# A graph network layer in 52 units of 40 steps: three jobs of the unit boundary put into earlier steps

## The chip, the cores and the metric

The kernel runs on one core of one Trainium2 chip. The metric is the device time of one launch in microseconds (us). Five engines of the core take part, each with its own instruction stream: PE (the matrix engine), ACT (activations), DVE (elementwise work), POOL (it starts the gathers) and SP (it starts the other transfers). Streams meet only in semaphores: an instruction waits until a counter has reached a number, and everything behind it on its engine waits with it.

## What is computed

One gated graph layer over 12,500 nodes with 128 features and 400,000 edges sorted by their destination. Cut to what matters:

```
h = relu(layernorm(x))
att = sigmoid(h[src] @ W_att[:d] + h[dst] @ W_att[d:] + b_att)
messages = (h[src] @ W_msg + b_msg) * att
aggregated = segment_sum(messages, dst, num_segments=num_nodes)
gi = aggregated @ W_ih.T + b_ih;   gh = h @ W_hh.T + b_hh
r = sigmoid(i_r + h_r);  z = sigmoid(i_z + h_z);  n = tanh(i_n + r * h_n)
h_new = (1 - z) * n + z * h
out = x + gamma * (h_new - mean) * rsqrt(var + BN_EPS) + beta
```

## The kernel before

**Stages.** A first part normalizes x, makes a table of messages and scores per node (98 tiles of 128 nodes, kept in SBUF as `m_all`), and sorts out the edges. A long middle, in units, sums messages and makes the new states. A last part applies the batch norm and stores.

**Two ways of summing.** The edges of the first 5,972 destinations go a tile of 128 edges at a time (1,520 tiles): POOL gathers the rows of the sources, ACT makes their gates (`gate(t)`, L928), DVE masks them to a window of destinations (`mask(t)`, L1217), PE multiplies (`scatter(t)`, L1491). The other 51 blocks of 128 destinations go "dense": ACT makes a gate for every pair of a source tile h and the block's destinations (`dense_gate`, L932, 98 tiles per block, into one of two large buffers), PE builds counts of edges from one-hot rows (`build`, L1501, sixteen pair groups per block), DVE multiplies gates by counts (`keep_pairs`, L1243, sixteen per block), and PE sums 98 products over the whole table (`block_part`, L1506; each shows as two MATMUL rows). DVE then copies the block's sum out of PSUM (`keep_block`, L1249, into `agg_blk`).

**Jobs.** A cell job turns 128 summed nodes into new states: six products on PE (`gru`, L1512 to L1515, twelve rows), two sigmoids on ACT (`gru_rz`, L937, L938), two operations on DVE (`gru_u`, L1254, L1257), a tanh on ACT (`gru_n`, L942), four operations on DVE (`gru_new`, L1262 to L1268). There are 51 dense jobs and 47 of gathered nodes. All use one PSUM bank, so that PE's products of a job wait until `gru_u` of the job ahead has read its own.

**Units and steps.** The middle is 52 units of 40 steps. Every engine runs through the same units and steps by its own loop, and tables of steps say what it does where; no engine waits for another at a step's end, so they are at different steps at one time. In unit u, PE builds the counts of block u and sums block u - 1. The order within a step is that of the code. What stands at the end of a unit and at the start of the next, before the change:

- PE: parts of block u - 1 in the 36 steps from `PARTS_AT` = 3 on, to step 38. Builds in steps 0, 2, 5, 7, ... 35, 37. A tile's `scatter` in about three steps of four, none in step 0. Cell jobs start in the steps of `GRU_AT` = (2, 10, 18, 26, 33); the dense one is in the first of these five places, a gathered one mostly in the fifth. The first part waits for all sixteen `keep_pairs` of its block and for the copy of the sum before it.
- DVE: `keep_pairs` of group 14 in step 39 and of group 15 in step 1 of the next unit, right behind the copy `keep_block`. `gru_u` of the fifth place's job (`U_AT` = 40) in step 0 of the next unit, behind step 0's other work.
- ACT: gates of the next block in steps 7 to 39 and 0 to 2 (`DENSE_AT` = 7, 36 parts), so none in steps 3 to 6. Part i of the gates waits until PE has summed part i of the block that used the buffer before: at step 7 + i ACT waits for what PE does at step 3 + i.
- SP loads keys, scores and h rows behind what frees their buffers, and in the last two units parts of x as the parts of the sum free the large buffers.

The planner gives the fifth place a job in 40 of the 52 units; units 0, 1, 2, 6, 14, 18, 25, 29, 33, 41, 45 and 51 have none there. Below, a crossing is the stretch from the last product of a block to the first of the next; "with a job" means that the unit that ends there had one in the fifth place (39 crossings between sums), "jobless" that it had none (ten, into units 2, 3, 7, 15, 19, 26, 30, 34, 42 and 46).

Of the kernel before, what the change touches and what calls it, by code (L numbers as in the profile page):

```python
# [19 lines left out]
BLOCKS = 51  # L20
UNITS = BLOCKS + 1
STEPS_U = 40
# [11 lines left out]
BEATS = PAIRS_B // BATCH  # L34
PER_BEAT = STEPS_U // BEATS
PARTS = 36
PARTS_AT = 3
DENSE_AT = 7
SET_LAG = 2
ADDED_LAG = SET_LAG + GROUPS_S  # L40
GRU_AT = (2, 10, 18, 26, 33)
RZ_AT = (8, 16, 23, 32, 39)
U_AT = (10, 18, 25, 34, 40)
N_AT = (13, 21, 28, 37, 43)
# [21 lines left out]
def tile_at(u, s):  # L66

    t = tiles_before(u, s)
    return t if tiles_before(u, s + 1) > t else None
# [22 lines left out]
def gru_jobs(steps):  # L92

    jobs, at, gathered = [], {}, 0
    for u in range(UNITS):
        for slot, s in enumerate(GRU_AT):
            if slot in ((4,) if u == BLOCKS else (1, 3)):
# [41 lines left out]
def gnn_program(nc, x, src, dst, W_msg, b_msg, W_att, b_att, W_ih, b_ih, W_hh, b_hh, gamma, beta, out):  # L139
# [30 lines left out]
    assert TILES % 2 == 1 and SPARSE < TILES and FINE <= P and GROWS <= P and HI <= P and 5 * GROWS <= 512 and KEYS <= 256  # L170
    assert SPARSE % SET == 0 and GROUPS % 2 == 0 and DENSE_AT + PARTS < STEPS_U + 4 and NEW_BACK_AT > NEW_AT[0] and PARTS_AT + PARTS < STEPS_U and SETS > 2 and TILES % 16 == 5
    assert QCOLS == 2 * QHALF and (FINE + 1) * QHALF <= 512 and FINE * P <= QCOLS * P
# [18 lines left out]
    with ExitStack() as ctx:  # L191
# [288 lines left out]
        def group_bases(first, n, engine):  # L480
            _, values = nc.values_load_multi_w_load_instructions(
                group_at[0:1, bass.ds(first, n)], engines=[engine], min_val=0, max_val=D0,
                skip_runtime_bounds_check_because=BOUNDED)
            return list(values)

        def set_ready(engine, k):

            engine.wait_ge(set_loaded[k % 2], 16 * (2 + GROUPS_S) * (k // 2 + 1))

        def keys_ready(engine, b):  # L490

            engine.wait_ge(keys_loaded[b % 2], 32 * (b // 2 + 1))
# [17 lines left out]
        def job_at(u, s, steps):  # L510

            for slot, step in enumerate(steps):
                v = u - (step // STEPS_U)
                if s == step % STEPS_U and (v, slot) in JOB_AT:
                    return JOB_AT[v, slot]
            return None
# [13 lines left out]
        def _(sp):  # L530
# [115 lines left out]
            def load_x_again(c):  # L646
                if width_of(c) == CHUNK:
                    sp.dma_start(x_again[:, c * TPC:(c + 1) * TPC, :], x_rows(c)).then_inc(x_back, 16)
                else:
                    for j, n in tiles_of(LAST):  # L650
                        sp.dma_start(x_again[0:n, c * TPC + j, :], x[c * CHUNK + j * P:c * CHUNK + j * P + n, :]
                                     ).then_inc(x_back, 16)

            def free_part(b, end):

                h = -(-(end - (LN_AT, KEY_AT)[b % 2]) // P)
                return next(i for i in range(PARTS) if slices_of(i, HI).stop >= h)

            def x_parts(b, s):

                chunks = range(X_EARLY) if b == BLOCKS - 2 else range(X_EARLY, CHUNKS)
                return [c for c in chunks if free_part(b, X_AT + (c + 1) * CHUNK) + PARTS_AT == s]

            for u in range(UNITS):
# [6 lines left out]
                for s in range(STEPS_U):  # L671
# [10 lines left out]
                    for c in x_parts(u - 1, s) if u >= BLOCKS - 1 else ():  # L682
                        sp.wait_ge(block_parts, PARTS * (u - 1) + s - PARTS_AT + 1)
                        load_x_again(c)
# [339 lines left out]
        def _(dve):  # L1024
# [184 lines left out]
            def next_batch(u, beat):  # L1209

                b, batch = (u, beat + 1) if beat + 1 < BEATS else (u + 1, 0)
                return (b, batch) if b < BLOCKS else None
# [14 lines left out]
            def set_bases(k):  # L1227

                return group_bases(k * GROUPS_S, GROUPS_S, ENGINE.DVE)

            def keep_set(k):

                dve.wait_ge(tiles_summed, (k + 1) * SET)
                wait_reuse(dve, groups_added, k * GROUPS_S)
                nc.vector.tensor_copy(lanes[:, :], ps[:, SP_BANK, 0:GROUPS_S * WIN]).then_inc(sums_kept, 1)
# [9 lines left out]
            def keep_block(b):  # L1245
                dve.wait_ge(block_parts, b * PARTS + PARTS)
                if ("dense", b - 1) in JOBS:
                    dve.wait_ge(gru_summed, JOBS.index(("dense", b - 1)) + 1)
                nc.vector.tensor_copy(agg_blk[:, :], ps[:, AM_BANK, 0:P]).then_inc(block_kept, 1)  # L1249
# [27 lines left out]
            for u in range(UNITS):  # L1277
                builds = u < BLOCKS
                for s in range(STEPS_U):
                    beat, i = s // PER_BEAT, s % PER_BEAT  # L1280
                    t = tile_at(u, s)
                    if t is not None:
                        if t % SET == 0:
                            set_ready(dve, t // SET)
                        if t % SET == SET_LAG - 1 and t > SET:
                            keep_set(t // SET - 1)
                        mask(t)
                        if t > SET and SET_LAG <= t % SET < ADDED_LAG:
                            of = t % SET - SET_LAG
                            add_group((t // SET - 1) * GROUPS_S + of, bases[of])  # L1290
                    if u == BLOCKS and s == LAST_TILES + SET_LAG:
                        keep_set(SETS - 1)
                        for of, base in enumerate(bases):
                            add_group((SETS - 1) * GROUPS_S + of, base)
                    if s == 1 and u > 1:
                        keep_block(u - 2)
                    if i == 1 and beat and builds:
                        keep_pairs(u, 2 * beat - 1)
                    if s == 1 and u:
                        keep_pairs(u - 1, 2 * BEATS - 1)  # L1300
                    if builds and i in (2, 3) and next_batch(u, beat):
                        b, batch = next_batch(u, beat)
                        if i == 2:
                            if batch == 0:
                                keys_ready(dve, b)
                            wait_reuse(dve, pairs_built, u * (2 * BEATS) + 2 * beat)
                            lo_hots(b, batch)
                        else:
                            key_hots(b, batch)
                    if i == 4 and builds:  # L1310
                        keep_pairs(u, 2 * beat)
                    if t is not None and t % SET == SET - 1:
                        bases = set_bases(t // SET)
                    k = job_at(u, s, U_AT)
                    if k is not None:
                        gru_u(k, nodes_of(k)[1])
                    k = job_at(u, s, NEW_AT)
                    if k is not None:
                        gru_new(k, nodes_of(k)[1], new_at(k), entry_of(k))
                    if u == 0 and s == 20:  # L1320
                        dve.wait_ge(bad_summed, 1)
                        nc.vector.tensor_copy(bad_all[:, :], ps[0:1, 7, 0:1]).then_inc(bad_known, 1)
                    if u == 0 and STEPS_U - 8 <= s < STEPS_U:
                        if s == STEPS_U - 8:
                            dve.wait_ge(edges_kept, ALL_TURNED)
                            for half in range(2):
                                dve.wait_ge(dense_stored[half], 32)
                                dve.wait_ge(scores_stored[half], 16)
                        n = -(-(AGG_W - ZEROED) // 8)
                        first = ZEROED + (s - STEPS_U + 8) * n  # L1330
                        nc.vector.memset(agg[:, first:min(AGG_W, first + n)], 0.0).then_inc(agg_zeroed, 1)
                if u == 0:
                    dve.wait_ge(agg_zeroed, 8)
# [79 lines left out]
        def _(pe):  # L1413
# [116 lines left out]
            for u in range(UNITS):  # L1530
                for s in range(STEPS_U):
# [3 lines left out]
                    if u < BLOCKS and s % PER_BEAT in (0, 2):  # L1535
                        build(u, 2 * (s // PER_BEAT) + (s % PER_BEAT) // 2)
                    if u and s == PARTS_AT:
                        pe.wait_ge(pairs_kept, u * (2 * BEATS))
                        wait_reuse(pe, block_kept, u - 1)
                    if u and PARTS_AT <= s < PARTS_AT + PARTS:  # L1540
                        for h in slices_of(s - PARTS_AT, HI):
                            last = block_part(u - 1, h)
                        last.then_inc(block_parts, 1)
                    k = job_at(u, s, GRU_AT)
                    if k is not None:
# [68 lines left out]
```

## Time and profile before

| | |
|---|---|
| median of 3 runs | 2234.89 us (2234.73 to 2235.26) |
| the profiled execution | 2235.2 us, span of its instructions 2233.5 us |
| busy in the span | PE 2037.2 us (91%), DVE 2007.9 us (90%), ACT 1977.8 us (89%), POOL 1534.1 us (69%) |
| granted TensorE clock, mean | 0.967 |
| the units | from about 262 to 2202 us |

A share of the span is a mean over the three stages; in the middle all of PE, ACT and DVE are busier than that. A matmul's end in the trace is modelled, and matmuls are pipelined, so the starts of PE's rows tell more than their durations. Of ACT and DVE the rows of successive instructions overlap by some 0.1 us; the distance between starts is what one costs.

### The profile page before, as it was taken

How to read it: one execution, taken by the hardware profiler on the slowest of the kernel's cores; microseconds unless marked ns; L12 is line 12 of the kernel's file. 1: busy time of each engine (PE TensorE's matmuls, PEld its weight loads, DVE VectorE, ACT ScalarE, POOL GpSimd, SP SyncE). 2: the span in 40 equal slices, each digit the busy share in tenths (PEclk: the TensorE clock that was granted, in tenths of full speed). 3: DMA queues.
4: the chain of work that ended last, by engine and by line, in shares of the span. 5: the costliest groups of instructions: out<-in, count | busy, mean ns of one | idle time of the engine just before them, and what ended most of it. 6: DMA issues, size and time to landing. Idle time of an engine off the chain costs nothing.

```text
span 2233.5 us, 53581 instructions
## 1 busy us (share of the span) xinstructions
PE 2037.2 (91%) x18022; PEld 1975.7 (88%) x18022; DVE 2007.9 (90%) x4463; ACT 1977.8 (89%) x6922; POOL 1534.1 (69%) x1618
## 2 busy tenths in 40 slices
PE   4535999999999999999999999999999999999997
PEld 4524999999999999999999999999999999999997
DVE  4966989999999999999999999999999999999985
ACT  1369899999999999999999999999999999999944
POOL 4575776777777777777777777677777777777760
PEclk9765999999999999999999999999999999999999
DMA  6862222222222222223222232222222222222255
GB/s 159 231 186 65 59 59 63 64 62 64 64 65 62 62 63 63 63 60 65 62 63 62 63 65 61 64 63 64 64 64 62 63 63 61 67 60 63 61 163 182
DMA packets 169059, 174.20 MB, mean 78 GB/s; under 512 B 80657, under 2 KB 132675, under 8 KB 168531
## 3 DMA queue, kind: packets, MB, share of 16 engines
q0 software_dynamic: 51136, 105.61, 20.9%
q1 hardware_dynamic: 114852, 61.60, 10.9%
q10 hardware_dynamic: 2796, 3.56, 0.8%
q8 instruction: 145, 2.38, 0.5%
q14 instruction: 130, 1.06, 0.2%
HBM read 143.99 MB, written 26.62 MB: 76 GB/s over the span
## 4 chain that ended last, share of the span: by engine, by line
PE 35%; ACT 35%; DVE 23%; issue 6%; DMA 1%; ACTq 0%; DVEq 0%
ACT big L932 27%; PE ps L1506 20%; DVE big L1243 7%; ACT gate_ring L928 6%; PE ps L1491 6%; PE ps L1501 5%; DVE gate_ring L1217 3%; DVE key_hot L1202 3%; DVE lo_hot L1194 2%; PE ps L1512 1%; PE ps L1513 1%; DVE big L1160 1%; DVE big L1147 1%; DVE h_blk L1264 1%; DVE big L1405 1%
## 5 line engine op out<-in xcount | busy, mean ns | idle before, releaser
L804 POOL DMA_INDIRECT row_ring<-node_table,set_idx x1520 | 1446.5, 952 | 578.8 <-issue 322.8
L932 ACT ACTIVATE big<-set_score,big 128x128 f32<-128x128 f32 x4998 | 1607.2, 394 | 82.6 <-PE ps L1506 82.2
L1506 PE MATMUL ps<-big 128*128 128x128 f32 x9996 | 1422.8, 281 | 0.0
L1506 PEld LDWEIGHTS ps<-big 128*128 128x128 f32 x9996 | 1238.9, 192 | 0.0
L1243 DVE TENSOR_TENSOR big<-ps,big 128x784 f32<-128x784 f32 x816 | 787.1, 965 | 8.8 <-ACT big L932 5.2
L1491 PE MATMUL ps<-gate_ring,row_ring 128*128 128x64 f32 x3040 | 541.5, 263 | 74.3 <-DVE gate_ring L1217 64.6
L1491 PEld LDWEIGHTS ps<-gate_ring,row_ring 128*128 128x128 f32 x3040 | 464.0, 194 | 117.6 <-DVE gate_ring L1217 99.8
L1217 DVE SCALAR_TENSOR_TENSOR gate_ring<-lane,set_rel,gate_ring 128x64 f32<-128x64 f32 x1520 | 420.7, 278 | 123.7 <-ACT gate_ring L928 117.8
L928 ACT ACTIVATE gate_ring<-set_win,row_ring 128x64 f32<-128x64 f32 x1520 | 506.6, 341 | 21.6 <-DMA row_ring<-node_table,set_idx 17.7
L1501 PE MATMUL ps<-key_hot,lo_hot 128*128 128x196 bf16 x3264 | 418.0, 251 | 17.2 <-DVE key_hot L1202 9.7
L1202 DVE TENSOR_TENSOR key_hot<-ps,set_key 128x1568 bf16<-128x1568 bf16 x408 | 393.6, 965 | 0.0
L1501 PEld LDWEIGHTS ps<-key_hot,lo_hot 128*128 128x128 bf16 x3264 | 310.2, 110 | 23.6 <-issue 20.5
L1194 DVE TENSOR_TENSOR lo_hot<-ps,set_lo 128x1024 bf16<-128x1024 bf16 x408 | 278.0, 681 | 6.9 <-DMA set_key<-dense_key 6.9
L1512 PE MATMUL ps<-h_blk,gates 128*128 128x128 f32 (+1 forms) x392 | 79.5, 286 | 0.5 <-DVE agg_blk L1249 0.5
L1462 PE MATMUL ps<-ident,big 128*128 128x128 f32 x98 | 20.5, 344 | 52.4 <-DVE big L1160 52.4
L883 ACT ACTIVATE big<-ps 128x512 f32<-128x512 f32 (+1 forms) x25 | 14.7, 589 | 55.4 <-issue 26.3
L1462 PEld LDWEIGHTS ps<-ident,big 128*128 128x128 f32 x98 | 13.7, 174 | 56.1 <-DVE big L1160 38.6
L1512 PEld LDWEIGHTS ps<-h_blk,gates 128*128 128x128 f32 x392 | 61.8, 199 | 0.7 <-issue 0.6
L937 ACT ACTIVATE n_blk<-ps,small 128x128 f32<-128x128 f32 (+1 forms) x98 | 34.4, 351 | 25.7 <-PE ps L1515 22.3
L1471 PE MATMUL ps<-big 128*128 128x130 f32 x196 | 36.6, 346 | 10.5 <-ACT big L883 10.4
L789 POOL DMA_INDIRECT big<-in_dst_dram,big x26 | 26.0, 1001 | 29.3 <-DVE big L1072 21.7
L942 ACT ACTIVATE n_blk<-n_blk,b_gates 128x128 f32<-128x128 f32 (+1 forms) x98 | 38.9, 397 | 6.5 <-DVE n_blk L1257 6.5
(131 smaller groups left out, 940.9 us busy)
## 6 DMA issues: line engine op xcount, KB each, us to landing
row_ring<-node_table,set_idx POOLq DMA_INDIRECT x1520
big<-in_x_dram SPq DMA_DIRECT2D x48, 256.0 KB, 6.0
h_blk<-hT_spill SPq DMA_DIRECT2D x97, 64.0 KB
node_table<-big SPq DMA_DIRECT2D x24, 258.0 KB
hT_spill<-big SPq DMA_DIRECT2D x24, 256.0 KB
out_dram<-big SPq DMA_DIRECT2D x24, 256.0 KB
set_win<-dst_scores SPq DMA_DIRECT2D x152, 32.0 KB
set_score<-dst_scores SPq DMA_DIRECT2D x51, 64.0 KB
```

What stands on the lines that cost most here:

```text
L804: nc.gpsimd.indirect_dma_start(row_ring[:, t % ROWS_RING, :], None, table, bass.IndirectOffsetOnAxis(ap=set_idx[:, t // SET % 2, t % SET:t ...
L928: nc.scalar.activation(gate_ring[:, t % GATES_RING, :], set_win[:, t // SET % 2, t % SET // GROUP, :], ACT.Sigmoid, bias=row_ring[:, t % R ...
L932: return nc.scalar.activation(a_buf[b % 2][:, h, :], set_score[:, b % 2, :], ACT.Sigmoid, bias=m_all[:, h, D:ROW])
L942: nc.scalar.activation(n_blk[:, 0:w], n_blk[:, 0:w], ACT.Tanh, bias=b_gates[:, 2:3]).then_inc(n_done, 1)
L1194: nc.vector.tensor_tensor(lo_hot[:, batch % 2, :, :, :], ps_lane_lo.bitcast(BF16).rearrange("p (l w) -> p l w", w=2).unsqueeze(1).broadcas ...
L1202: nc.vector.tensor_tensor(key_hot[:, batch % 2, :, :, :], ps_lane_key.bitcast(BF16).rearrange("p (h w) -> p h w", w=2).unsqueeze(1).broadc ...
L1217: nc.vector.scalar_tensor_tensor(out=hot, in0=lane[:, :], scalar=set_rel[:, t // SET % 2, t % SET:t % SET + 1], in1=hot, op0=ALU.is_equal, ...
L1243: nc.vector.tensor_tensor(a, ps_quad(q), a, ALU.mult).then_inc(pairs_kept, 1)
L1491: nc.tensor.matmul(ps_window(g), row_ring[:, t % ROWS_RING, 0:D], gate_ring[:, t % GATES_RING, :], start=t % GROUP == 0, stop=t % GROUP == ...
L1501: last = nc.tensor.matmul(ps_pairs(q, j), lo_hot[:, batch % 2, t // 2, :, t % 2], key_hot[:, batch % 2, t, :, :], start=True, stop=True)
L1506: return nc.tensor.matmul(ps[:, AM_BANK, 0:P], m_all[:, h, 0:D], a_buf[b % 2][:, h, :], start=h == 0, stop=h == HI - 1)
L1512: nc.tensor.matmul(both, gates[:, 3 + g, :], h, start=True, stop=False)
```

## The change

Four edits. The 36 parts start in step 2 instead of 3 and end in step 37. The first place of the cell jobs is step 0 instead of 2. `keep_pairs` of group 15 is in step 0 instead of 1. `keep_block` is in step 39 of the unit that sums the block, at the end of the step, instead of step 1 of the next.

```diff
-PARTS_AT = 3
+PARTS_AT = 2
...
-GRU_AT = (2, 10, 18, 26, 33)
+GRU_AT = (0, 10, 18, 26, 33)
...
-                    if s == 1 and u > 1:
-                        keep_block(u - 2)
                     if i == 1 and beat and builds:
                         keep_pairs(u, 2 * beat - 1)
-                    if s == 1 and u:
+                    if s == 0 and u:
                         keep_pairs(u - 1, 2 * BEATS - 1)
...
                     if t is not None and t % SET == SET - 1:
                         bases = set_bases(t // SET)
+                    if s == STEPS_U - 1 and 0 < u < BLOCKS:
+                        keep_block(u - 1)
                     k = job_at(u, s, U_AT)
                     if k is not None:
                         gru_u(k, nodes_of(k)[1])
```

ACT's and POOL's streams stay as they are, and the list of cell jobs and of who does what in which place stays too. On SP one load of a part of x in the second last unit stands one place earlier.

DVE at the crossing into unit 21, from step 38 on. `lo_hot` and `key_hot` are the one-hot rows, `big<-ps,big` with 98x8 is `keep_pairs`, `gate_ring` the mask of a tile. Before:

```order
L1202 TENSOR_TENSOR key_hot<-ps,set_key 128x1568
L1217 SCALAR_TENSOR_TENSOR gate_ring<-lane,set_rel,gate_ring 128x64
L1243 TENSOR_TENSOR big<-ps,big 128x98x8
L1254 SCALAR_TENSOR_TENSOR n_blk<-ps,b_gates,n_blk 128x128
L1257 TENSOR_TENSOR n_blk<-ps,n_blk 128x128
L1217 SCALAR_TENSOR_TENSOR gate_ring<-lane,set_rel,gate_ring 128x64
L1249 COPY agg_blk<-ps 128x128
L1243 TENSOR_TENSOR big<-ps,big 128x98x8
L1217 SCALAR_TENSOR_TENSOR gate_ring<-lane,set_rel,gate_ring 128x64
L1194 TENSOR_TENSOR lo_hot<-ps,set_lo 128x1024
```

DVE at the same place after the change:

```order
L1202 TENSOR_TENSOR key_hot<-ps,set_key 128x1568
L1217 SCALAR_TENSOR_TENSOR gate_ring<-lane,set_rel,gate_ring 128x64
L1243 TENSOR_TENSOR big<-ps,big 128x98x8
L1249 COPY agg_blk<-ps 128x128
L1243 TENSOR_TENSOR big<-ps,big 128x98x8
L1254 SCALAR_TENSOR_TENSOR n_blk<-ps,b_gates,n_blk 128x128
L1257 TENSOR_TENSOR n_blk<-ps,n_blk 128x128
L1217 SCALAR_TENSOR_TENSOR gate_ring<-lane,set_rel,gate_ring 128x64 x2
L1194 TENSOR_TENSOR lo_hot<-ps,set_lo 128x1024
```

The copy and the last `keep_pairs` now stand ahead of `gru_u` and of the masks of steps 1 and 2.

PE at the same crossing, from step 37's tile on before the change (`ps<-big` are parts of the sum, `key_hot,lo_hot` a build, `h_blk` and `agg_blk` the dense cell job). Before:

```order
L1491 MATMUL ps<-gate_ring,row_ring 128x64
L1501 MATMUL ps<-key_hot,lo_hot 128x196 x4
L1506 MATMUL ps<-big 128x128 x3
L1491 MATMUL ps<-gate_ring,row_ring 128x64
L1506 MATMUL ps<-big 128x128 x3
L1491 MATMUL ps<-gate_ring,row_ring 128x64
L1501 MATMUL ps<-key_hot,lo_hot 128x196 x4
L1491 MATMUL ps<-gate_ring,row_ring 128x64 x2
L1501 MATMUL ps<-key_hot,lo_hot 128x196 x4
L1512 MATMUL ps<-h_blk,gates 128x128
```

and then the other products of the job, a tile and five parts. After, again from step 37's tile:

```order
L1491 MATMUL ps<-gate_ring,row_ring 128x64
L1501 MATMUL ps<-key_hot,lo_hot 128x196 x4
L1506 MATMUL ps<-big 128x128 x3
L1491 MATMUL ps<-gate_ring,row_ring 128x64 x2
L1501 MATMUL ps<-key_hot,lo_hot 128x196 x4
L1512 MATMUL ps<-h_blk,gates 128x128
L1513 MATMUL ps<-agg_blk,gates 128x128
L1512 MATMUL ps<-h_blk,gates 128x128
L1513 MATMUL ps<-agg_blk,gates 128x128
L1514 MATMUL ps<-h_blk,gates 128x128
L1515 MATMUL ps<-agg_blk,gates 128x128
L1491 MATMUL ps<-gate_ring,row_ring 128x64 x2
```

and then a build and two parts. Ahead of the job stand the tiles of steps 38 and 39 and one build, behind it the tiles of steps 1 and 2 and the other build; the same pieces as before lie between the last and the first part, in another order.

## Rows read from the trace of the kernel before

**Rows 1.** The source view of the copy, L1249: its engine's idle time.

```profile
L1249 DVE COPY agg_blk<-ps x51: 281/283/293, 261.6 to 2201.7; 128x128 f32<-128x128 f32 x51
...
  PE ps L1506: 6.0, 2
```

**Rows 2.** Five stretches, 300 to 2130 us: sum of busy time by engine.

```profile
sum 1830.00, PE 1768.62 PEld 1726.76 DVE 1712.72 ACT 1755.22 POOL 1316.52; mean PE 353.72 PEld 345.35 DVE 342.54 ACT 351.04 POOL 263.30
```

**Rows 3.** Waits from 300 to 2150 us: total us, times, longest.

```profile
ACT big L932 <- PE ps L1506: 74.1, 49, 3.3
...
PE ps L1491 <- DVE gate_ring L1217: 48.4, 85, 1.0
```

**Rows 4.** DVE's timeline at a typical crossing (start, us, what, count, [idle before]).

```profile
885.39 0.35 DVE L1254 SCALAR_TENSOR_TENSOR n_blk<-ps,b_gates,n_blk 128x128 f32<-128x128 f32 x1
885.77 0.29 DVE L1257 TENSOR_TENSOR n_blk<-ps,n_blk 128x128 f32<-128x128 f32 x1
886.51 0.28 DVE L1217 SCALAR_TENSOR_TENSOR gate_ring<-lane,set_rel,gate_ring 128x64 f32<-128x64 f32 x1 [0.44 <-ACT gate_ring L928]
886.71 0.28 DVE L1249 COPY agg_blk<-ps 128x128 f32<-128x128 f32 x1
886.91 0.96 DVE L1243 TENSOR_TENSOR big<-ps,big 128x784 f32<-128x784 f32 x1
887.79 0.28 DVE L1217 SCALAR_TENSOR_TENSOR gate_ring<-lane,set_rel,gate_ring 128x64 f32<-128x64 f32 x1
```

**Rows 5.** PE's timeline at the same crossing, last part to first part.

```profile
885.22 0.89 PE L1506 MATMUL ps<-big 128*128 128x128 f32 x6
885.95 0.33 PE L1491 MATMUL ps<-gate_ring,row_ring 128*128 128x64 f32 x2
886.12 0.51 PE L1501 MATMUL ps<-key_hot,lo_hot 128*128 128x196 bf16 x4
886.85 0.43 PE L1491 MATMUL ps<-gate_ring,row_ring 128*128 128x64 f32 x2 [0.23 <-DVE gate_ring L1217]
888.12 0.43 PE L1491 MATMUL ps<-gate_ring,row_ring 128*128 128x64 f32 x2 [0.84 <-DVE gate_ring L1217]
...
890.27 1.33 PE L1506 MATMUL ps<-big 128*128 128x128 f32 x10
```

**Rows 6.** The timeline at a tight crossing, into unit 21.

```profile
1003.45 0.89 PE L1506 MATMUL ps<-big 128*128 128x128 f32 x6
...
1004.37 0.29 DVE L1249 COPY agg_blk<-ps 128x128 f32<-128x128 f32 x1
...
1007.94 1.33 PE L1506 MATMUL ps<-big 128*128 128x128 f32 x10
```

**Rows 7.** The chain that ended last, behind that crossing: PE comes back into it.

```profile
1020.72 0.43 PE ps L1491 x2
```

**Rows 8.** The timeline at a jobless crossing, into unit 30.

```profile
1351.68 0.89 PE L1506 MATMUL ps<-big 128*128 128x128 f32 x6
...
1352.15 0.97 DVE L1243 TENSOR_TENSOR big<-ps,big 128x784 f32<-128x784 f32 x1
...
1353.85 0.28 DVE L1249 COPY agg_blk<-ps 128x128 f32<-128x128 f32 x1
...
1354.39 0.33 ACT L928 ACTIVATE gate_ring<-set_win,row_ring 128x64 f32<-128x64 f32 x1
...
1354.93 0.27 DVE L1217 SCALAR_TENSOR_TENSOR gate_ring<-lane,set_rel,gate_ring 128x64 f32<-128x64 f32 x1
...
1357.94 0.69 ACT L932 ACTIVATE big<-set_score,big 128x128 f32<-128x128 f32 x2 [1.62 <-PE ps L1506]
```

**Rows 9.** PE at that crossing: its first part.

```profile
1357.23 0.61 PE L1506 MATMUL ps<-big 128*128 128x128 f32 x4
```

**Rows 10.** Windows with the granted clock (the 0.50 or 1.00 ahead of the DMA share).

```profile
301.75:305.16 3.41, 3.41 (x19) 3.41 (x18) 3.41 (x8) 0.64 (x3) 1.15 (x3) 0.50 0.42 58
...
2134.70:2138.12 3.42, 3.42 (x19) 3.38 (x19) 3.35 (x10) 1.06 (x5) 2.00 (x2) 0.50 0.18 39
```

## The prediction

> **What bounds the kernel now.** I read the page first. Its shares of the span (PE 91%, DVE 90%, ACT 89%) name no single engine, so I cut out the units: between 300 and 2130 us PE is busy 1768.6 of 1830 us, ACT 1755.2, DVE 1712.7 [rows 2], which leaves them 61, 75 and 117 us of idle time. One copy of a block's sum follows the other by (2201.7 - 261.6) / 50 = 38.8 us [rows 1]; that is the time of a unit. The view of waits then says where the idle time lies. ACT waited 49 times, once per crossing, for a part of PE's sum, 74.1 us in all, 1.5 us each; PE waited 85 times for a mask of DVE, 48.4 us in all [rows 3]. At the typical crossing PE's two waits of this kind are 0.23 and 0.84 us [rows 5]: 49 times 0.84 is 41 us, so that nearly all of PE's visible waiting stands at the crossings too.
>
> The timeline of one crossing shows the loop. PE's last part ends at 885.22 + 0.89 = 886.11 [rows 5]. DVE could not copy the sum then: it stood before the mask of step 1, which waited 0.44 us for ACT's gate; the copy came at 886.71, `keep_pairs` of group 15 at 886.91, the mask of step 2 at 887.79 [rows 4]. PE, idle 0.84 us, took that mask at 888.12, built, did the cell job and began the new sum at 890.27 [rows 5]. Only a part of that sum lets ACT go on with the gates of its step 7. Through all 51 copies DVE waited for PE's last part only twice [rows 1]; at the tight crossing the copy follows the end of the last part (1004.34) by 0.03 us [rows 6], at the typical one by 0.60. Behind the tight crossing the chain of work that ended last runs over DVE, and PE comes back into it only at 1020.72 [rows 7]: DVE is the late one for the first third of a unit. So the bound is a loop through all three engines, closed at the crossing, and no engine's throughput.
>
> **The change, crossings with a job (39).** Nothing is added or removed; every instruction is there before and after, and DVE's, PE's and ACT's work per unit stay the same. What moves is who waits. Let E be the end of a block's last part.
>
> Before, the first new part starts at E + 4.16 in the typical crossing (890.27 - 886.11) and at E + 3.60 in the tight one (1007.94 - 1004.34) [rows 5, 6]. Going through the crossings I count some ten of 39 at the tight end, so the mean is about 0.75 x 4.16 + 0.25 x 3.60 = 4.02.
>
> After, DVE reaches the copy early (its `keep_pairs` of group 14 was over by 885.39, when `gru_u` began [rows 4]) and has to wait for E. Then: copy at E + 0.03 [rows 6], group 15 0.20 later (886.71 to 886.91), the next instruction 0.88 later (886.91 to 887.79), and `gru_u` 0.38 + 0.29 until its end [rows 4]. That is E + 1.78. PE follows DVE's end by 0.05 (888.07 to 888.12) [rows 4, 5] and starts the cell job at E + 1.83. Behind the wait it has the same four pieces as before: job, two tiles, build. They took 890.27 - 888.12 = 2.15 [rows 5], of which up to 0.1 is the slow start of a product behind a wait; I take 2.10. The first new part starts at E + 3.93. The crossing itself gains 4.02 - 3.93 = 0.09 us. This is where the change looks larger than it is: the wait for a mask goes, but the dense job now stands behind `gru_u` of the job before it, through the shared PSUM bank, and `gru_u` now stands behind `keep_pairs` and the copy. Behind it on DVE are the masks of steps 1 and 2; PE needs them only after its job of some 1.4 us, so they cost nothing.
>
> A second term: where DVE is behind in the first third of a unit, PE stalls on masks. After the change DVE reaches any step later behind its copy by `gru_u` and one mask, 0.67 + 0.20 = 0.87 (0.20 is 886.51 to 886.71). PE reaches it later behind the copy by 3.90 - 3.56 (890.27 - 886.71) = 0.34 and by one more step of parts with its tile, 0.73 (885.95 - 885.22) and, three times in four, 0.17 (886.12 - 885.95) [rows 5], 0.86 in all. That is 1.2 against 0.87, so PE's stalls can shrink by 0.3. How long they are is not in one row, as the modelled ends hide up to 0.2 us of each; bounds 0 and 0.3, I take 0.25 since the chain runs through DVE there. Sum 0.34 x 39 = 13 us.
>
> **Jobless crossings (10).** Here no `gru_u` is in the way. In the one shown E is 1351.68 + 0.89 = 1352.57; DVE is free of group 14 at 1352.15 + 0.88 = 1353.03, so the copy is at 1353.03 instead of 1353.85. Group 15 follows at 1353.23, mask 1 at 1354.11, and mask 2 once ACT's gate is ready, at 1354.39 + 0.33 = 1354.72; with 0.04 until DVE starts and 0.28 for the mask PE goes on at 1355.1. Its job has by then been done, in the time in which it now waits; tile 0.17 and build 0.35 give the first part at 1355.6, against 1357.23 [rows 8, 9]. ACT's 1.62 us of waiting [rows 8] would vanish. But DVE's mask of step 2 is only 0.17 earlier (1354.76 against 1354.93), and PE, one step of parts further on (about 0.86), meets DVE in the first third of the unit: that lets 0.17 + 0.86 = 1.03 through. Between 1.03 and 1.62 I take 1.1, 11 us for ten.
>
> **The clock.** In five stretches of 3.41 us each, the first and last of which are shown, the granted clock was 0.50 [rows 10], the lower level of 1.2 GHz. Four of the five follow jobless crossings, after PE had stood nearly idle for longer than elsewhere. ACT's longest wait, at such a crossing, was 3.3 us [rows 3] instead of 1.62, so that one fall costs 1.7 us. With the cell job pulled into PE's gap of the jobless crossings these four should go: 4 x 1.7 = 7 us.
>
> **Costed at nothing.** The first and last units and the one x load that moves are taken as zero, within 2 us. The earlier copy needs PSUM's sum only, and `agg_blk` is free: the job that reads it was done in step 0.
>
> **The sum.** 13 + 11 + 7 = 31 us. The profiled execution is 2235.2 us, its span 2233.5; it is 0.3 above the median of 2234.89. 2235.2 - 31 = 2204 us.
>
> **Rivals.**
> - *Forecast, chance 0.54.* The terms at their bounds: crossings with a job 0 to 0.45 us each (0 to 18), jobless 1.0 to 1.6 (10 to 16), clock 3 to 8 (the fifth fall too). 2235 - 13 to 2235 - 42: 2193 to 2222.
> - *No difference, 0.16.* If most crossings behave like the tight one, where DVE already had the sum at once, the crossing with a job is longer by 3.93 - 3.60 = 0.33 us, 39 times 13 us, and what the jobless ones and the clock give back (18) is eaten up: 2231 us. For it: a kernel in which DVE waits for E each time has no slack left there. Against it: 0.60 us lay between E and the copy at the typical crossing.
> - *Slower, 0.13: the clock falls at the crossings with a job.* PE's waits there were two, 0.23 and 0.84, with a tile between [rows 5]. Afterwards they are one: it has two tiles and a build (until about E + 0.6) and then nothing until E + 1.83, 1.2 to 1.3 us. If the clock fell at each, 39 x 1.7 = 66 us, and the time is 2204 + 66 = 2270. It decides from 31 / 1.7 = 18 falls on. Against it: the typical crossing with its 1.1 us of waiting, and most with somewhat more, held 1.00, and the job's twelve products now break up the thin stretch. The Trainium skill ("TensorE: Matmul & The Clock Gate", "A second HAM failure mode: psum-queue depth-cycling") says that a matrix engine which idles briefly between groups of products again and again can swing between the two clocks. By that rule a regular gap at each unit would be this rival; the trace agrees only so far that the falls follow the longest gaps.
> - *Larger gain, 0.12.* ACT's wait of 74.1 us in 49 crossings [rows 3] is the ceiling of what the loop can give. If the stalls in the units shrink as well, and the loop closes on ACT's own work, 50 to 60 of it come: 2180 us.
> - The remaining 0.05 is for what I don't see, above all work near the sets' ends on DVE.
>
> **How the numbers follow.** What a measurement of this kernel can tell from no change is 0.2%, 4.5 us. Faster: the forecast, the larger gain, and a third of the second rival, 0.72. Same: most of the rest of that rival, 0.13. Slower: the clock and what I don't see, 0.15. The range takes in the larger gain and the weaker terms but not the clock: 2182 to 2228. The likeliest case's own is 2193 to 2222.
>
> **What would show it.** Right: DVE's copy waits for L1506 at nearly every crossing, 0.4 to 0.8 us each; PE's wait for a mask at the crossing is gone and one of about 1.3 us before L1512, put down to `gru_u` (L1257), stands there 39 times; ACT's wait for L1506 falls from 74 to about 45 us and is near zero at jobless crossings; the distance of copies is near 38.2 us; fewer than three windows of clock 0.50 within the units. Wrong: copies that start without waiting mean that DVE and not PE is last; stretches of 0.50 at the crossings with a job mean the clock; a wait of PE for masks in steps 7 to 18 longer than now means that DVE, later by 0.87 us, became the bound.

## The result and the profile after

The changed kernel took 2207.35 us in the median of 4 runs (2205.89 to 2207.76), the kernel before 2234.81 (2233.95 to 2235.26). The ratio is 0.9878, 95% interval 0.9866 to 0.9890: 27.5 us less. The forecast was 2204 in 2182 to 2228. The profiled execution has a span of 2205.5 us, 28.0 less than before.

The view of waits of the changed kernel, 300 to 2150 us (total, times, longest), answers to [rows 3]:

```profile
PE ps L1512 <- issue: 46.0, 40, 1.2
ACT big L932 <- PE ps L1506: 38.0, 45, 1.8
...
DVE agg_blk L1249 <- PE ps L1506: 15.8, 23, 1.6
PE ps L1491 <- DVE gate_ring L1217: 9.1, 34, 0.5
ACT n_blk L937 <- DVE bn_all L1268: 7.7, 12, 2.8
```

ACT's wait for a part of the sum went from 74.1 to 38.0 us, PE's wait for masks from 48.4 to 9.1. In their place stands a new one, 40 times before the first product of the dense job (L1512), 46 us in all. The view puts it down to "issue", that is to nothing it can see; the timeline below shows that the job starts 0.10 us after `gru_u` ends, and in the trace of e11_parts3 the view names `gru_u` (L1257) for the same wait.

The windows view, sum of five stretches from 300 to 2130 us, answers to [rows 2]:

```profile
sum 1830.00, PE 1765.57 PEld 1735.49 DVE 1731.93 ACT 1767.89 POOL 1336.97; mean PE 353.11 PEld 347.10 DVE 346.39 ACT 353.58 POOL 267.39
```

In the same 1830 us ACT and DVE are busy for 13 and 19 us more, PE's idle time is 64 us against 61. The engines do the same work in less time.

A crossing with a job, into unit 13, answers to [rows 4, 5]. The rows are from three timelines, of DVE, then PE, then ACT:

```profile
680.22 0.97 DVE L1243 TENSOR_TENSOR big<-ps,big 128x784 f32<-128x784 f32 x1
682.08 0.29 DVE L1249 COPY agg_blk<-ps 128x128 f32<-128x128 f32 x1 [0.89 <-PE ps L1506]
682.29 0.96 DVE L1243 TENSOR_TENSOR big<-ps,big 128x784 f32<-128x784 f32 x1
683.17 0.34 DVE L1254 SCALAR_TENSOR_TENSOR n_blk<-ps,b_gates,n_blk 128x128 f32<-128x128 f32 x1
683.55 0.29 DVE L1257 TENSOR_TENSOR n_blk<-ps,n_blk 128x128 f32<-128x128 f32 x1
...
681.19 0.86 PE L1506 MATMUL ps<-big 128*128 128x128 f32 x6
...
683.94 0.46 PE L1512 MATMUL ps<-h_blk,gates 128*128 128x128 f32 x2 [1.16 <-issue]
...
685.75 0.50 PE L1501 MATMUL ps<-key_hot,lo_hot 128*128 128x196 bf16 x4
...
686.82 0.69 ACT L932 ACTIVATE big<-set_score,big 128x128 f32<-128x128 f32 x2 [1.40 <-PE ps L1506]
```

The chain is the forecast one: last part over at E = 681.19 + 0.86 = 682.05, copy at E + 0.03, group 15 at + 0.24, `gru_u` over at + 1.79, cell job at + 1.89. There are 40 crossings of this kind, not 39: one into each of the units 4 to 51 that follows a unit with a job in the fifth place. The time from E to the first part is 4.04 us in their median (3.82 to 4.15), against 4.02 (3.29 to 6.43) before. It got no shorter, only uniform.

A jobless crossing, into unit 30 (DVE, then PE, then ACT), answers to [rows 8, 9]:

```profile
1335.35 0.96 DVE L1243 TENSOR_TENSOR big<-ps,big 128x784 f32<-128x784 f32 x1
1336.23 0.28 DVE L1249 COPY agg_blk<-ps 128x128 f32<-128x128 f32 x1
...
1337.96 0.29 DVE L1217 SCALAR_TENSOR_TENSOR gate_ring<-lane,set_rel,gate_ring 128x64 f32<-128x64 f32 x1 [0.38 <-ACT gate_ring L928]
...
1334.30 0.85 PE L1506 MATMUL ps<-big 128*128 128x128 f32 x6
...
1336.46 0.50 PE L1501 MATMUL ps<-key_hot,lo_hot 128*128 128x196 bf16 x4 [0.54 <-DVE big L1243]
1336.80 0.41 PE L1512 MATMUL ps<-h_blk,gates 128*128 128x128 f32 x2
...
1338.92 1.30 PE L1506 MATMUL ps<-big 128*128 128x128 f32 x10
...
1339.65 0.69 ACT L932 ACTIVATE big<-set_score,big 128x128 f32<-128x128 f32 x2
```

ACT goes on at its step 7 without any wait; before it had stood 1.62 us. The copy follows group 14 at once, as forecast.

The granted clock, in the first and the last of the five windows that make up the sum above:

```profile
300.00:700.00 400.00, 386.14 (x3563) 379.39 (x3562) 378.46 (x812) 388.97 (x1387) 291.80 (x309) 1.00 0.29 64
...
1900.00:2130.00 230.00, 221.39 (x2047) 217.72 (x2046) 217.91 (x467) 210.34 (x749) 169.52 (x179) 1.00 0.30 68
```

The third figure from the end, 1.00, is the clock. It is 1.00 in all five: none of the five stretches at 0.50 of [rows 10] is left between the first and the last sum.

**Where the 28 us came from.** Measured from the last part of one block to the last part of the next, that is over a crossing and the stretch of parts behind it, a unit behind a crossing with a job took 38.51 us in the mean before and 38.27 after (40 of them: 9.7 us), behind a jobless one 40.12 and 38.32 (ten: 18.0 us). The first block's last part came 0.3 us earlier. Ten of the fifty crossings thus gave two thirds of the gain.

### The profile page after: what moved, and what is told of

Same layout as the page of the kernel before. It is cut to its first block, busy times and chain, and to the rows that moved or that the text cites. A ratio compares the mean times of both kernels' runs of the same rounds, so it can differ in the third digit from the quotient of the medians.

```text
span 2205.5 us, 53581 instructions
## 1 busy us (share of the span) xinstructions
PE 2008.8 (91%) x18022; PEld 1961.2 (89%) x18022; DVE 2002.0 (91%) x4463; ACT 1980.0 (90%) x6922; POOL 1535.1 (70%) x1618
## 4 chain that ended last, share of the span: by engine, by line
PE 35%; ACT 34%; DVE 23%; issue 7%; DMA 1%; ACTq 0%; DVEq 0%
ACT big L932 25%; PE ps L1506 20%; DVE big L1243 6%; ACT gate_ring L928 6%; PE ps L1491 5%; PE ps L1501 5%; DVE key_hot L1202 3%; DVE gate_ring L1217 3%; DVE lo_hot L1194 2%; PE ps L1512 1%; PE ps L1513 1%; DVE big L1160 1%; DVE h_blk L1264 1%; DVE big L1147 1%; DVE big L1405 1%
## 5 line engine op out<-in xcount | busy, mean ns | idle before, releaser
L1506 PE MATMUL ps<-big 128*128 128x128 f32 x9996 | 1417.5, 281 | 0.0
L1506 PEld LDWEIGHTS ps<-big 128*128 128x128 f32 x9996 | 1236.5, 192 | 0.0
L1243 DVE TENSOR_TENSOR big<-ps,big 128x784 f32<-128x784 f32 x816 | 787.4, 965 | 9.6 <-ACT big L932 5.2
L1491 PE MATMUL ps<-gate_ring,row_ring 128*128 128x64 f32 x3040 | 516.0, 259 | 29.2 <-DVE gate_ring L1217 24.1
L1491 PEld LDWEIGHTS ps<-gate_ring,row_ring 128*128 128x128 f32 x3040 | 456.6, 194 | 53.3 <-DVE gate_ring L1217 45.3
L1512 PE MATMUL ps<-h_blk,gates 128*128 128x128 f32 (+1 forms) x392 | 79.0, 283 | 46.5 <-issue 46.0
L1512 PEld LDWEIGHTS ps<-h_blk,gates 128*128 128x128 f32 x392 | 59.3, 191 | 54.6 <-issue 54.6
L937 ACT ACTIVATE n_blk<-ps,small 128x128 f32<-128x128 f32 (+1 forms) x98 | 34.7, 354 | 31.1 <-PE ps L1515 23.3
```

What stands on the lines that cost most here:

```text
L1243: nc.vector.tensor_tensor(a, ps_quad(q), a, ALU.mult).then_inc(pairs_kept, 1)
L1491: nc.tensor.matmul(ps_window(g), row_ring[:, t % ROWS_RING, 0:D], gate_ring[:, t % GATES_RING, :], start=t % GROUP == 0, stop=t % GROUP == ...
L1506: return nc.tensor.matmul(ps[:, AM_BANK, 0:P], m_all[:, h, 0:D], a_buf[b % 2][:, h, :], start=h == 0, stop=h == HI - 1)
L1512: nc.tensor.matmul(both, gates[:, 3 + g, :], h, start=True, stop=False)
```

## The experiments

Two theories were put on record once the result was known, each time before the run that tests them. **T**: the chain over the crossing (last part, copy, group 15, `gru_u`, job, first part) sets the unit. **M**: the loop is longer; DVE's work *behind* the copy, up to where PE or ACT needs DVE in the new unit, then PE's parts up to the last one, sets it, and a shorter crossing alone gives nothing. The changed kernel agrees with both.

This table is worked out from the starts and ends of the parts (L1506) in the traces of the kernels below. A crossing runs from a block's last part to the next block's first, the stretch from there to that block's last part; means in us.

| | before | changed | e9_u39 | e10_u39first | e11_parts3 |
|---|---|---|---|---|---|
| with a job (40): crossing | 4.01 | 4.04 | 3.18 | 2.86 | 4.17 |
| the stretch behind it | 34.50 | 34.22 | 34.99 | 35.11 | 34.65 |
| both | 38.51 | 38.27 | 38.16 | 37.98 | 38.82 |
| jobless (ten): crossing | 5.43 | 3.87 | 3.90 | 3.89 | 3.67 |
| the stretch behind it | 34.68 | 34.45 | 34.45 | 34.46 | 35.10 |
| both | 40.12 | 38.32 | 38.35 | 38.35 | 38.77 |

The trace of e8_after, the changed kernel once more, has the means of "changed" within 0.03 us.

Of the twelve runs four fell on a chip on which the kernel before takes 2237 us, as in the comparison; eight fell on others, where it took 2618 to 2658 us, and where PE has many more waits that the trace puts down to nothing (last section). The four on the first chip decide; the others are told behind them.

### The four that decide: the changed kernel and three variants on one chip

**e8_after**, the changed kernel itself.

> The changed kernel itself, beside the kernel before on a chip of today, where the kernel before takes 2618 to 2658 us instead of 2235: PE's rows there show waits of 0.3 to 1.9 us put down to nothing, and the clock at 0.50 some 30 to 40 times within the units. If the crossing's chain is what the change works on, the crossings with a job stay near 4.0 us at the least and the jobless ones fall to about 3.5, and the ratio to before stays below 1, but by less than 1.2%, since PE's own waits now set most of the unit: 0.985 to 1.00.

Measured: 2206.77 us, ratio to before 0.9866 (0.9849 to 0.9882). The chip was not one of the slow ones, so that the condition in the text did not hold; the run repeats the result of the comparison.

**e9_u39**: `gru_u` of the fifth place in step 39, behind the copy.

```diff
-U_AT = (10, 18, 25, 34, 40)
+U_AT = (10, 18, 25, 34, 39)
```

> gru_u in step 39 behind the copy, on the same chip as e8_after. Theory T (the crossing's chain sets the unit): faster than e8_after by up to 0.9 us a crossing, 1.6% of the unit where no other wait covers it. Rival M (DVE's work behind the copy sets it): the least crossing falls to about 3.1 us, the time is that of e8_after within 0.3%.

Measured: 2202.65 us, ratio to before 0.9851 (0.9834 to 0.9867), 4 us below e8_after and within its interval. The least crossing is 2.94 us and the median 3.16, as expected, 0.88 below 4.04; had T held, 35 us would have gone. By the table the crossing is 0.86 us shorter in the mean and the stretch behind it 0.76 longer. Part of the reason is in the waits, 300 to 2150 us:

```profile
ACT n_blk L937 <- DVE bn_all L1268: 31.3, 39, 2.8
...
ACT big L932 <- PE ps L1506: 11.2, 23, 1.0
```

ACT's wait for the first part fell from 38.0 to 11.2 us, and its wait for DVE rose from 7.7 to 31.3: 45.7 together in the changed kernel, 42.5 here. L937 is the first sigmoid of the dense job, in step 8; it may not overwrite `n_blk` before `gru_new` of the job before (L1268, DVE's step 5) is through. PE meets DVE too: of its waits for masks, those between 10.5 and 16 us behind the first part are 2.6 us in all before the change, 6.8 in the changed kernel and 8.2 here. T falls. M stands, with the addition that DVE is met twice: by ACT at step 8, and by PE at its masks.

**e10_u39first**: the same, but `gru_u` ahead of the copy.

```diff
-U_AT = (10, 18, 25, 34, 40)
+U_AT = (10, 18, 25, 34, 39)
...
-                    if s == STEPS_U - 1 and 0 < u < BLOCKS:
-                        keep_block(u - 1)
                     k = job_at(u, s, U_AT)
                     if k is not None:
                         gru_u(k, nodes_of(k)[1])
+                    if s == STEPS_U - 1 and 0 < u < BLOCKS:
+                        keep_block(u - 1)
```

> gru_u in step 39 ahead of the copy, on the same chip. Theory T: faster than e9_u39 by 0.2 to 0.4 us a crossing. Rival M: faster than e8_after by up to 0.4 us a crossing, 0.7%, though e9_u39 is not.

Measured: 2196.4 us, ratio to before 0.9820 (0.9803 to 0.9836), 10.4 us below e8_after, 0.26 a job crossing. This is what M asks for: 0.67 us of DVE's work is put where DVE waited. Its waits:

```profile
ACT n_blk L937 <- DVE bn_all L1268: 34.2, 39, 2.8
...
DVE agg_blk L1249 <- PE ps L1506: 5.0, 11, 1.0
```

DVE's wait before the copy fell from 15.6 us (in e8_after) to 5.0, and that is the 10 us. M's own number, 0.4 us a crossing, took the mean wait of 40 crossings, but half of them have next to none to give. This kernel is faster than the changed one and than e9_u39.

**e11_parts3**: the changed kernel with the parts in steps 3 to 38.

```diff
-PARTS_AT = 2
+PARTS_AT = 3
```

> The parts in steps 3 to 38 again, the rest as changed, on the same chip. Theory T: 5 us slower than e8_after, 0.2%. Rival M: 0.8 us a unit slower, up to 40 us, 1.5%.

Measured: 2235.19 us, ratio to before 0.9991 (0.9981 to 1.0000): 28.4 us above e8_after. The crossing with a job grew by 0.20 us only in the median (to 4.24), which is T's share; crossing and stretch together grew by 0.55 in the mean. Its waits:

```profile
ACT big L932 <- PE ps L1506: 68.9, 55, 2.0
...
PE ps L1512 <- DVE n_blk L1257: 54.0, 39, 1.4
DVE agg_blk L1249 <- PE ps L1506: 32.6, 38, 1.3
```

The copy now waits for the last part 32.6 us instead of 15.6, since PE has one more step of parts behind the masks on which it met DVE. So the three other edits together give nothing measurable in the sum, and the gain appears with the first one.

In the sum only, for the table shows two parts that cancel. Against the kernel before, the three edits make a unit behind a jobless crossing 1.35 us shorter (40.12 to 38.77, ten: 13.5 us) and one behind a crossing with a job 0.31 us longer (38.51 to 38.82, forty: 12.3 us). The first edit then takes 0.55 us from each of the forty and 0.45 from each of the ten. The clock is 1.00 through the units of this kernel too, without any stretch at 0.50, so that what the four falls behind jobless units had cost is among the 13.5 us.

What the first edit gives alone is not known from this chip, and the move of the dense job to step 0 (`GRU_AT`) was run nowhere by itself. With the first edit each part also comes one step earlier against the gates with which ACT refills the buffer. That this is not the gain is argued only: e9_u39 takes most of ACT's wait for parts away and gets 4 us.

### On the slower chips

Their times are told as ratios to the kernel before on the same chip. In the order e4, e6, e1, e2, then e5, e7, then e12, e13, the kernel before itself took 2617.86 us there for the first four, 2658.32 and 2652.46 for the next two, 2657.56 for the last two.

**e4_u39**, the same kernel as e9_u39.

> The changed kernel, with gru_u of the fifth place's job in step 39, right behind the copy, instead of step 0 behind keep_pairs of group 15. Theory T (the chain over the crossing sets the unit: end of the last part, copy, group 15, gru_u, cell job, first part, 4.04 us): group 15 leaves the chain, the crossing falls by 0.9 to about 3.1 us, and 39 crossings give up to 35 us: 2172 to 2180. Rival M (the loop is set by DVE's work between the copy and the masks of about step 15, where PE stalls 13 us behind the first part, and by PE from there to the last part): DVE's work behind the copy is the same, so the crossing gets shorter and the stall longer by as much; 2200 to 2207.

Measured: 2619.62 us, ratio 1.0010 (0.9997 to 1.0024). **e7_u39again**, once more:

> The same kernel as e4_u39 (gru_u of the fifth place's job in step 39, behind the copy), once more, since PE's rows of the first runs show waits of 0.3 to 1.2 us for nothing that the profile names, which neither kernel had in the traces of the comparison. Theory T (the chain over the crossing sets the unit): the crossing falls from 4.04 to about 3.1 us and the time to 2172 to 2180. Rival M (DVE's work behind the copy sets it): the crossing falls as well, but PE's stall 13 us behind the first part grows by as much; 2200 to 2207.

Measured: a single execution of each, 2657.12 against 2652.46 us, too little for a verdict. **e5_u39first**, the same kernel as e10_u39first:

> The changed kernel, with gru_u of the fifth place's job in step 39 ahead of the copy, so that DVE does it in the time in which it waits for the last part. Behind the end of the last part stand only the copy and group 15, and the cell job's products need no waiting: theory T, the crossing falls from 4.04 to about 2.9 us, 39 x 1.1 = up to 40 us: 2167 to 2180. Rival M (the loop runs over DVE's work behind the copy to the masks of about step 15, and PE from there): DVE's work behind the copy is shorter by gru_u's 0.67 us, of which the time in which it now waits for the last part (0.4 us in the mean) is free: 39 x 0.4 = 16 us, 2188 to 2195, with a longer stall of PE 13 us behind the first part.

Measured: 2647.39 us, ratio 0.9964 (0.9949 to 0.9978). **e6_parts3**, the same as e11_parts3:

> The changed kernel, but the parts of the sum are in steps 3 to 38 again; the other three edits stay. Theory T: only the tile of step 3 is added to the crossing, 0.13 us x 40 = 5 us: 2212. Rival M: behind the mask at which PE stalls it has one more step of parts until the last part, about 0.8 us per unit, so up to 31 us: 2225 to 2238.

Measured: 2652.12 us, ratio 1.0140 (1.0122 to 1.0159). The order of the variants is the one found above (`gru_u` first, `gru_u` behind the copy, parts in step 3), the distances to the kernel before are not: all are some 1.5% worse against it than on the other chip. The changed kernel was not run there; whether its gain holds on such a chip is open. If it stood to these variants as on the other chip, its ratio would be about 1.00, an estimate from these three distances, and nothing of the gain would be left.

**e1_copy39**: the kernel before with only the copy moved.

```diff
-                    if s == 1 and u > 1:
-                        keep_block(u - 2)
...
+                    if s == STEPS_U - 1 and 0 < u < BLOCKS:
+                        keep_block(u - 1)
```

> The kernel before, with nothing but the copy moved to the end of step 39. DVE then waits for the last part ahead of gru_u, the mask of step 1 and group 15. The mask of step 2 comes about 0.3 us later at a typical crossing and 0.9 later at a tight one: about +0.45 x 39 = 18 us, 2245 to 2260, by both theories. If DVE's order at the crossing did not matter: 2235.

Measured: 2636.06 us, ratio 1.0074 (1.0057 to 1.0090), 18 us slower.

**e2_pairs0**: the kernel before with only group 15 in step 0.

```diff
-                    if s == 1 and u:
+                    if s == 0 and u:
```

> The kernel before, with nothing but keep_pairs of group 15 moved to step 0. DVE does it in the time in which it waited 0.44 us for the gate of step 1, so all that follows comes about 0.45 us earlier: -0.45 x 39 and 0.17 x 10, about -19 us, 2216, by both theories. If only the whole set of edits helps: 2235.

Measured: 2614.7 us, ratio 0.9986 (0.9974 to 0.9999): 3 us less, at most 7 by the interval, where 19 were expected. The signs of both are the expected ones, and the loss of e1_copy39 has its size; but with PE's own waits in every unit neither number can be carried to the other chip.

**e12_parts2**: the kernel before with only `PARTS_AT = 2`.

```diff
-PARTS_AT = 3
+PARTS_AT = 2
```

> The kernel before with nothing but the parts in steps 2 to 37; copy and group 15 stay in step 1, the dense job in step 2, now behind that step's parts. Theory M (the loop of DVE's work behind the copy, PE from the mask of about step 15 to the last part): PE has one step of parts less behind that mask, -0.8 us a unit, DVE has 0.87 us less behind the copy than in the changed kernel, and the job's 1.36 us leave the crossing, which falls from 4.0 to about 2.7: the loop loses more than in the changed kernel, until ACT's own work (1.4 us a unit below the time before) stops it: 2175 to 2205. Rival S (the four edits need each other, since the part in step 2 waits for the copy and group 15 of step 1 on DVE): no better than the kernel before, 2225 to 2240.

Measured: 2666.37 us, ratio 1.0037 (1.0022 to 1.0052). **e13_parts2_pairs0**, with group 15 in step 0 as well:

> As e12_parts2, with group 15 in step 0 as well, so that DVE does it while it would wait for the gate of step 1. Theory M: up to 0.4 us a unit below e12_parts2, less where ACT's work already sets the unit: 2170 to 2200 and not slower than e12_parts2. Rival S: this one gives what e12_parts2 does not, 2205 to 2215.

Measured: 2652.16 us, ratio 0.9979 (0.9964 to 0.9993). Both numbers look like rival S, which says that the first edit needs the others. It is not shown: between the first and the last copy of a sum the granted clock was at 0.50 in 51 and 43 stretches, against 28 to 42 in the others of these chips and none in the four that decide, and the kernel before has no trace there. Nor is the 0.50 a full answer, since e1_copy39 has 42 such stretches, nearly as many as e13_parts2_pairs0. Whether the earlier parts alone would do on an undisturbed chip stays open.

## Why the prediction was right, and where it was not

**The bound.** "A loop through all three engines, closed at the crossing, and no engine's throughput" held, but not as "closed at the crossing": e9_u39 and e10_u39first show that the loop runs on behind it.

**Crossings with a job.** The chain was right instruction by instruction: 1.83 us to the cell job forecast, 1.89 measured; 2.10 for the rest, 2.15. The sum was 3.93 against a measured 4.04, so that the term of -0.09 us a crossing came out as +0.02. The prediction counts the same four pieces of PE in every crossing; that holds for the typical one, but in 16 of the 40 a tile less stood there before, and in one after, so that 0.38 tiles of 0.17 us moved into the crossing in the mean. The warning of that step, that the wait for a mask goes and one for `gru_u` comes, is the 46.0 us at L1512. The prediction's 39 should be 40, which changes its sum by 0.3 us.

**The second term, -0.25 us** (PE's stalls on masks behind the crossing). The stretch behind these crossings got 0.27 us shorter in the mean (34.50 to 34.22), of which 0.06 is the tile that left it. So the size is right, and part of the reason: one step of parts less behind DVE's masks. But the prediction made it a side term and gave the crossing the space, and e11_parts3 shows that without this edit a unit is 0.55 us longer. Nor did all stalls shrink: PE's waits for masks outside the crossings rose from 3.6 to 7.9 us, most of them 11 to 15 us behind the first part. That is the last of the signs named as "wrong", DVE late in steps 7 to 18. It came, at a size that cost nothing in the sum.

**Jobless crossings.** Forecast 11 us and 7 for the clock, 1.8 us each; measured 18.0 in ten, 1.80 each. ACT's wait is gone as said: 1.60 to 1.74 us at the six without a fall of the clock, 0 to 0.23 after. These six gained 1.24 us each (0.6 to 2.0), near the forecast 1.1, but not by the way described: the first part was to start at E + 3.03 (1355.6 - 1352.57) in the one shown and started at E + 3.77, because the build ahead of the job waited 0.54 us for a `keep_pairs` (L1243) and the job was not done when mask 2 was. The crossings of the six gave 0.94 us in the mean instead of some 1.6, the stretches behind them 0.30. That the two errors meet near 1.1 is in part luck.

**The clock.** All five falls went. The price of 1.7 us can be read from the trace of before. Into unit 19, with the clock at 0.50, and into unit 30, at 1.00, PE goes from the same tile through build and job to its first part:

```profile
926.60 0.69 PE L1491 MATMUL ps<-gate_ring,row_ring 128*128 128x64 f32 x2 [0.97 <-DVE gate_ring L1217]
...
930.26 1.33 PE L1506 MATMUL ps<-big 128*128 128x128 f32 x10
...
931.02 1.30 ACT L932 ACTIVATE big<-set_score,big 128x128 f32<-128x128 f32 x4 [3.25 <-PE ps L1506]
...
1355.26 0.43 PE L1491 MATMUL ps<-gate_ring,row_ring 128*128 128x64 f32 x2 [0.84 <-DVE gate_ring L1217]
```

That is 3.66 us against 1.97 (first part at 1357.23, [rows 9]), 0.17 of it for one tile more: 1.5 us for the clock. ACT's waits at the four such crossings are 3.23 to 3.27 us against 1.60 to 1.74. Of this about 1.4 us reached the unit: the four gained 2.63 us each, the six others 1.24, and 4 x 1.4 is 5.6 us where 7 was forecast. In e11_parts3 the difference is the same, 2.27 against 0.73. The fifth fall was at a crossing with a job, into unit 50, whose unit gained 1.1 us where the other 39 gained 0.22 in the mean; it is in the first term's 9.7 us.

**The sum.** 13 + (11 + 7) forecast, 9.7 + 18.0 measured, and 0.3 ahead of the first crossing.

**The signs that were named.** DVE's copy follows the end of the last part by 0.04 us in 35 of 40 crossings with a job, so it does wait nearly always; but the view counts only 23 waits over its threshold, of 0.7 us each: half of them are next to nothing, where 0.4 to 0.8 was said. ACT's wait for L1506 fell to 38 us (45 was said), PE's before L1512 came as said, 40 times 1.15 us. The copies stand 38.26 us apart, where 38.2 was said.

**The rivals.** "No difference" priced the job crossings at +0.33 us against the tight ones; the crossing did become as long as that (4.04 against 3.60) for those. With the first edit it did not matter. Without it the rival is what happened: e11_parts3 loses 12.3 us at the crossings with a job, where the rival said 13, gains 13.5 at the jobless ones, where it said 18, and stands at the time of before. The larger gain did not come: ACT still waits 45.7 us, for PE's parts and for DVE together. The clock did not fall: PE's single idle time of 1.16 us held 1.00 all through. On the slower chips this rival is real: in e4_u39 PE waits 24 times for more than 1.5 us before the first product of a job, and at 19 of these a stretch at 0.50 begins within 2.5 us of the job's start.

## What to carry to other kernels

Where several engines run through one table of steps, a wait at the seam is the end of a loop and not its cause: before shortening the chain across it, look for the next place where an engine meets the late one. Taking 0.9 us out of the seam gave 4 us in 40 passes because the wait moved to the next meeting; one step less of PE's work behind that meeting, on top of the three other edits, gave 28, and filling the late engine's own idle time gave 10 more. And a set of edits that gives nothing in the sum can hold a gain and a loss: sort the passes by kind before calling an edit without effect. An edit of the order is worth what it takes out of the late engine's or the last engine's part of the loop, not what it takes out of the visible wait.

## What the runs showed of the hardware that was not expected

On three of the four chips of the experiments the kernel before took 17 to 19% longer than in the comparison, in every execution. PE's timeline in e12_parts2 shows single products behind waits that the trace puts down to nothing, at distances of 0.7 us:

```profile
1101.71 0.30 PE L1491 MATMUL ps<-gate_ring,row_ring 128*128 128x64 f32 x1 [0.29 <-issue]
1102.41 0.22 PE L1491 MATMUL ps<-gate_ring,row_ring 128*128 128x64 f32 x1 [0.40 <-issue]
1103.13 0.92 PE L1506 MATMUL ps<-big 128*128 128x128 f32 x6 [0.50 <-issue]
```

Such waits come singly or in bursts, in e12_parts2 one every 9 us in the median. Between the first and the last copy the eight traces of these chips have 107 to 316 waits put down to "issue", those of the four that decide 40, 39, 0 and 1. The windows view of the same kernel shows what they do to the clock (the 0.94 ahead of the DMA share, against 1.00) and to all engines; the second fence is e10_u39first on the other chip:

```profile
1000.00:1500.00 500.00, 437.18 (x3655) 419.73 (x3654) 395.79 (x831) 405.51 (x1421) 299.04 (x317) 0.94 0.24 53
```

```profile
1000.00:1500.00 500.00, 490.35 (x4477) 479.20 (x4476) 476.31 (x1022) 489.47 (x1745) 366.71 (x388) 1.00 0.30 64
```

In 500 us PE gets through 3655 products there and 4477 here. The durations of single instructions are the same within 4% in the traces of these chips and the other (`keep_pairs` 967 to 969 ns on all four), and so are those of the packets of the busiest DMA queue (26 to 27 ns in the median). A shortage of instructions for PE would look like this, but that is a guess. What causes it was not found, and no experiment was made on it.
